# The exps of each block's first right chunk in two column parts

## The reference

```
xn   = group_norm(x)                       # 32 groups
g_x  = g_w @ xn + g_b                      # 128 channels, transposed to (n, 128)
f    = einsum('bnc,bcm->bnm', xn^T, xn)    # 4096 x 4096, symmetric
attn = softmax(f, axis=-1)
y    = attn @ g_x
wy   = W_w @ y + W_b
wy   = batch_norm(wy) * gamma + beta       # statistics over all 4 images
out  = x + (wy + xn)
```

## Time and profile before

| | |
|---|---|
| median of 3 runs | 2335.37 us (2332.52 to 2337.6) |
| the profiled execution's own time | 2335.4 us |
| its span, from first to last instruction | 2333.3 us |
| mean granted TensorE clock | 0.988 of full speed |
| PE busy | 2146.0 us, 92% |
| DVE busy | 1714.3 us, 73% |
| ACT busy | 1084.3 us, 46% |
| POOL busy | 904.7 us, 39% |

### The profile page before, as it was taken

One profiled execution on the slowest core, in us unless ns is written; L12 is line 12 of the kernel. 1 busy time (PEld: TensorE's weight loads), 2 busy tenths in 40 slices (PEclk: granted clock), 3 DMA queues, 4 the chain that ended last, 5 costly groups with the idle time before them and its releaser, 6 DMA issues.

```text
span 2333.3 us, 32462 instructions
## 1 busy us (share of the span) xinstructions
PE 2146.0 (92%) x9520; PEld 1507.4 (65%) x9520; DVE 1714.3 (73%) x3062; ACT 1084.3 (46%) x2206; POOL 904.7 (39%) x624
## 2 busy tenths in 40 slices
PE   5899999998999999998999999999899999999778
PEld 4787777654587776654568777765458777665323
DVE  5466667888856767788866666788985677777876
ACT  3344554454434454546444455445444444554435
POOL 3011224568601023459631122446860102346860
PEclk9899999999999999999999999999999999999999
DMA  3121233535412323454421223353441232346859
GB/s 134 71 95 73 102 107 118 194 113 169 147 43 87 112 87 113 149 172 136 162 68 80 89 86 119 122 193 114 160 156 51 77 113 93 107 142 205 297 203 360
DMA packets 108407, 304.55 MB, mean 131 GB/s; under 512 B 11456, under 2 KB 11968, under 8 KB 93888
## 3 DMA queue, kind: packets, MB, share of 16 engines
q1 hardware_dynamic: 108224, 302.37, 38.1%
HBM read 159.71 MB, written 142.61 MB: 130 GB/s over the span
## 4 chain that ended last, share of the span: by engine, by line
PE 63%; POOL 16%; issue 11%; DVE 5%; ACT 3%; DMA 2%; SPq 0%; DVEq 0%; POOLq 0%; ACTq 0%
PE bank L1109 9%; PE bank L1168 9%; PE bank L1111 9%; PE bank L1110 9%; PE bank L1144 8%; POOL fy_d L682 6%; POOL fy_c L682 6%; PE bank L1172 4%; PE bank L1174 4%; PE bank L1173 4%; PE bank L1304 2%; POOL xl L655 2%; PE bank L1234 2%; ACT ring L748 2%; DVE lacc L963 2%
## 5 line engine op out<-in xcount | busy, mean ns | idle before, releaser
L774 ACT CAST phi<-bank 128x512 fp32r<-128x512 f32 x480 | 280.4, 586 | 838.6 <-PE bank L1144 837.9
L911 DVE TENSOR_SCALAR_CACHE_REDUCE ring<-bank 128x512 f32<-128x512 f32 x576 | 395.5, 687 | 255.3 <-PE bank L1111 252.8
L1109 PE MATMUL bank<-xh 128*128 128x512 f32 x1152 | 541.2, 470 | 7.2 <-POOL xl L655 6.4
L1111 PE MATMUL bank<-xh,xl 128*128 128x512 f32 x1152 | 455.1, 395 | 0.0
L1110 PE MATMUL bank<-xl,xh 128*128 128x512 f32 x1152 | 452.3, 393 | 0.0
L946 DVE TENSOR_TENSOR plo<-bank,phi 128x512 fp32r<-128x512 f32 x480 | 325.6, 684 | 141.1 <-ACT phi L774 98.0
L1144 PEld LDWEIGHTS bank<-ident,ring 128*128 128x128 f32 x1920 | 234.0, 142 | 191.7 <-issue 126.2
L682 POOL TENSOR_TENSOR fy_c<-fy_c,maxrow 128x512 f32<-128x512 f32 x200 | 299.7, 1500 | 148.3 <-DMA fy_c<-spill 148.3
L682 POOL TENSOR_TENSOR fy_d<-fy_d,maxrow 128x512 f32<-128x512 f32 x188 | 280.9, 1497 | 193.6 <-DMA fy_d<-spill 193.6
L748 ACT ACTIVATE ring<-ring,nmax 128x512 f32<-128x512 f32 x480 | 344.5, 719 | 0.0
L1144 PE MATMUL bank<-ident,ring 128*128 128x128 f32 x1920 | 295.4, 277 | 52.3 <-ACT ring L748 24.2
(11 more groups left out here) (109 smaller groups left out, 2921.5 us busy)
## 6 DMA issues: line engine op xcount, KB each, us to landing
spill<-ring SPq DMA_DIRECT2D x112, 1024.0 KB, 4.4
fy_c<-spill SPq DMA_DIRECT2D x200, 256.0 KB, 4.3
fy_d<-spill SPq DMA_DIRECT2D x188, 256.0 KB, 4.3
ring<-x_dram SPq DMA_DIRECT2D x40, 512.0 KB, 4.5
lbuf<-spill SPq DMA_DIRECT2D x60, 256.0 KB, 3.7
yd<-yn SPq DMA_DIRECT2D x32, 256.0 KB, 3.2
fx_a<-x_dram SPq DMA_DIRECT2D x16, 512.0 KB, 6.7
out_dram<-fx_a SPq DMA_DIRECT2D x16, 512.0 KB, 4.4
```

What stands on the lines that cost most here:

```text
L774: nc.scalar.copy(phi[:, HI_BUF[n], :], whole(p)).then_inc(hi_made, 1)
L911: last = nc.vector.tensor_scalar(ring[:, SLOT[u], t, :], src, 1.0, None, ALU.mult, ALU.max, accum_out=rowm[:, t, c:c + 1])
L1109: nc.tensor.matmul(dst, xh[:, k, rows], xh[:, k, cols], start=(k == 0), stop=False)
L1111: last = nc.tensor.matmul(dst, xl[:, k, rows], xh[:, k, cols], start=False, stop=(k == K - 1))
```

## The change

The four exps of a block's first right chunk are issued in two column parts. Where the plan has the exp of row tile 0, all four row tiles' first 128 columns (the columns of tile r = 0) are now issued, four ACTIVATEs of 128x128; the other 384 columns of each row tile stay at the step that the plan gave it, behind them. Exps of later chunks stay whole, and are issued ahead of the parts within a step. The `turn` of tile r = 0 of such a chunk waits only for the four exps of 128 columns; the turns of r = 1 to 3 wait for those of 384 columns. The row sums of the second part go to a further column of `rsum`, which `sum_right` adds with the others (its slice is open at the end). All other work keeps its place in every engine's order.

```diff
+def first_right(j):
+    return j + 1 if turned_self(j, j) else j
...
-EXPS_AT = {s: [x for x in PRODUCTS if EXP_STEP.get(x) == s] for s in range(FIRST_EXP, TILES)}
-EXP_NO = {x: n for n, x in enumerate(x for s in range(FIRST_EXP, TILES) for x in EXPS_AT[s])}
+def exp_parts(s):
+    here = [x for x in PRODUCTS if EXP_STEP.get(x) == s]
+    whole = [(*x, slice(0, W)) for x in here if x[1] > first_right(x[0])]
+    opened = [x for x in here if x[1] == first_right(x[0])]
+    return whole, opened
+
+EXPS_AT = {}
+for _s in range(FIRST_EXP, TILES):
+    _whole, _opened = exp_parts(_s)
+    EXPS_AT.setdefault(_s, []).extend(_whole)
+    if _opened and _opened[0][2] == 0:
+        EXPS_AT[_s] += [(*_opened[0][:2], t, slice(0, P)) for t in range(T)]
+    EXPS_AT[_s] += [(*x, slice(P, W)) for x in _opened]
+EXP_NO = {(*x[:3], x[3].start): n for n, x in enumerate(x for s in range(FIRST_EXP, TILES) for x in EXPS_AT[s])}
...
+def exp_count(j, c, r):
+    start = 0 if c > first_right(j) or r == 0 else P
+    return max(EXP_NO[j, c, t, start] for t in range(T)) + 1
...
-        rsum = sb("rsum", [P, 2, T, NB])
+        rsum = sb("rsum", [P, 2, T, NB + 1])
...
-            def exp_right(b, j, c, t):
+            def exp_right(b, j, c, t, cols):
-                if t == 0:
+                if t == 0 and cols.start == 0:
                     act.wait_ge(max_made, b * NB + j + 1)
...
-                nc.scalar.activation(ring[:, SLOT[u], t, :], ring[:, SLOT[u], t, :], ACT.Exp,
-                                     bias=nmax[:, j % 3, t:t + 1], accum_out=rsum[:, j % 2, t, c:c + 1]
+                into = NB if cols.start else c
+                nc.scalar.activation(ring[:, SLOT[u], t, cols], ring[:, SLOT[u], t, cols], ACT.Exp,
+                                     bias=nmax[:, j % 3, t:t + 1], accum_out=rsum[:, j % 2, t, into:into + 1]
                                      ).then_inc(right_exp, 1)
...
-                pe.wait_ge(right_exp, b * NEXP + max(EXP_NO[j, c, t] for t in range(T)) + 1)
+                pe.wait_ge(right_exp, b * NEXP + exp_count(j, c, r))
```

## The result

The changed kernel is slower: 2395.7 us, where 2374 was forecast and 2390 was the upper end of the range. The ratio to the kernel before is 1.0252, 95% interval 1.0229 to 1.0274, or 59 us on 2336.3 us (the medians of the comparison). One of its four executions was in a slower state (3631.2 us at a mean clock of 0.555), which the median of 2395.7 counts and the ratio leaves out; the other three took 2391.9, 2393.7 and 2397.8 us. The profiled execution took 2391.9 us with a span of 2390.0 us, 56.7 us longer than before.

What follows compares the result with a forecast made beforehand. PE, busy 92% of the span, was taken as the bound, so time counts only where PE idles. 2335.4 + 24.6 (delays behind ACT's split exps) + 14.0 (clock) = 2374 us; range 2352 to 2390 us.

Steps and rivals of the forecast that it cites:

- the place: Starts of blocks 1 to 3: first turn 1.3 us earlier, but second turn, waiting for `plo`, 1.12 us later.
- the price of a part: On ACT, splitting an exp costs 0.28 us more per row tile, 1.12 us per chunk; ends 0.13 and 0.38 us.
- the delays: Later casts and `plo` at block starts: 13.4 + 4.9 + 3.8 + 2.5 = 24.6 us.
- Nothing, in eight places: Starts of blocks 5 and 7: ACT's idling before the next cast hides the added 1.22 us, so no delay.
- the clock's term: Starts of blocks 1 to 4: PE's joined idling of 2.5 to 2.9 us drops the clock, costing 14.0 us.
- I take two thirds of the 16, 11 drops, at 1.27 us: Blocks 1 to 4: 11 of 16 starts drop to 1.2 GHz, each costing 1.27 us, 14.0 us in all.
- My upper bound, 16 x 1.8 = 29 us: Clock loss at most: all 16 starts of blocks 1 to 4 drop, each at 1.8 us, dearest against cheapest stretch.
- Rival 1: Starts of blocks 1 to 4: slower by the 24.6 us, but the clock keeps up; 2360 us; chance 0.22.
- Rival 3: Part price at its upper end (34 us), nearly all 16 places lose the clock (29 us): 2398 us; chance 0.07.
- Rival 2: Part price near its lower end (11 us) and the clock holds: 2346 us; chance 0.08.
- rival 4: Faster: PE's 24.2 us of waiting for exps go, its `plo` waits don't grow: 2318 us; chance 0.04.
- rival 5: Effects cancel, or delays vanish in DVE's and POOL's waits in later blocks: 2335 us; chance 0.03.

Runs made afterwards that it cites:

- e8: Kernel before, whole exps, plus four one-column exps behind each first chunk's exps and unused matmuls where PE idles at blocks 1 to 4: 2361.3 us, ratio 1.0102.
- e3: Changed kernel plus ten unused 512-column matmuls on PE where it idles at each start of blocks 1 to 4: 2362.0 us, ratio 1.0094.
- e7: Changed kernel with the split only in blocks 5 and 7, whole exps elsewhere: 2341.7 us, ratio 1.0014 to the kernel before.
- e4: Changed kernel with ACT's cast of tile -1 (block 4: -2 and -1) moved ahead of the long parts, behind the short: 2359.6 us, ratio 1.0084.
- e2: Kernel before, whole exps, plus four one-column exps with accumulator behind the exps of each first chunk: 2382.1 us, ratio 1.0166.
- e1: Changed kernel, split kept, but the turn of tile 0 waits for all eight parts again: 2388.3 us, ratio 1.0203.

## Why the prediction was wrong

**Right: the place.** That the second turn and not the first sets the start of a block, that the wait for exps would turn into a wait for `plo`, and that the idling would be one stretch of 2.5 to 2.9 us: measured 2.65 to 2.81 (2.74 in most of blocks 1 to 3, 2.72 in most of block 4). The row of waits for `plo` reached 58.6 us, "over 50" as said; that for exps 9.7.

**Right: the price of a part.** 0.28 us from a difference of rows; e8 measured 0.28, the short and long exps 0.39 and 0.60 as worked out.

**Right in the main: the delays.** 24.6 us against 22 us in e3 (0.94%, interval 15 to 29 us) and 24 us in e8. Block by block, e3's marks move by 1.0 to 1.1 us at block 2, 0.8 to 1.1 at block 3 (1.12 forecast) and 1.1 at block 4 (1.22). In the changed kernel block 6 moves by 0.9 to 1.0 us in three images (1.12) and by 0.3 in the last (0.4), and the start of block 0 in the first image by 1.12 us, for 1.1. Its start between images can't be told from the clock's drops around it. Blocks 5 and 7 cost nothing at seven of eight starts, as e7 shows. "Nothing, in eight places" was wrong for one: block 7 of the last image costs 1.1 us. The idling of ACT that was to hide it had been read in another image.

**Wrong: the clock's term, 14.0 us.** The step "I take two thirds of the 16, 11 drops, at 1.27 us" failed on both factors, most on the second. There were 15 drops. Together they cost 34 us net (37 by the ratios), 2.2 us each. Counted by their length, 85 us at half clock, it would be 43 us; but e3, which lacks them, had 55 us of 1.2 GHz elsewhere and the changed kernel 42, so 2.2 us is if anything low.

I had read 1.27 us from two stretches that end with block 1's first exp. In both began a drop of 3.4 us, with PE busy all through it (start:end, length, busy us of five engines, granted clock, DMA):

```profile
181.47:184.88 3.41, 3.41 (x16) 3.01 (x15) 1.14 (x2) 1.69 (x5) 0.00 (x0) 0.50 0.01 5
737.84:741.25 3.41, 3.41 (x16) 3.02 (x15) 0.86 (x2) 0.58 (x1) 0.00 (x0) 0.50 0.02 7
```

The second cost 1.6 to 1.8 us, about half its length. The first cost 0.7 to 0.9: my row ended at 183.71, with 1.2 us of the low clock still to come, and what PE lost in these was taken up by its wait for the exps, 0.94 us before the first turn in place of 1.83. Behind the second turn of a block there is no such wait: PE was busy 6.80 us of 6.80 in the changed kernel's drop from 268.2, and 9.54 of 10.20 in that from 1968.0, and low clock cost up to half of its length. I also held a drop to be one short stretch; seven of 15 lasted 6.8 or 10.2 us. My upper bound, 16 x 1.8 = 29 us, was therefore no bound. With it and my price for the parts the sum would have been 2389 us, inside the range; with 34 us it is 2394. So the upper end of the range rested on the same step.

**The rivals.** Rival 1 (the clock keeps up) is what e3 made by hand, at 2362 us for 2360; it isn't what the chip did. The Trainium skill, in "TensorE: Matmul & The Clock Gate", its rules for kernel authors ("Why this matters for your kernels"), ties the fall of the clock to a longer gap than PE had here; the traces don't agree, with 15 drops at 16 stretches of 2.65 to 2.81 us in the changed kernel and four at 12 places of 1.5 us in e4. Rival 3 came nearest in time (2398), with the wrong reason for half of it: it needed 34 us from the parts, which cost 24. Rival 2 fell with the price, rival 4 with the row of waits for `plo`, which grew, and rival 5 with e3, where the delay stays with the clock up.

## What to carry to other kernels

Before splitting an instruction to release one waiter sooner, look at what stands behind it in its own engine's queue and at the waiter's next wait: here ACT owed PE a cast as well, each second part pushed it back by 0.28 us, and reordering what PE asks for, with the cast earlier too (1% gained), did what a quicker first answer did not. Price idle time of TensorE in front of dense work at more than its length: here 1.1 us more of it at each of 16 places cost another 34 us in clock, 2.1 us a place.

## What the runs showed of the hardware

A drop of the granted clock to 1.2 GHz did not always end with the first work behind it: it lasted 3.4 us in eight of 15 cases, and up to 10.2 us, with PE busy 9.54 us of them. Filling 2.3 us of PE's 2.74 us of idling with matmuls that nobody reads took away all 15 drops, and with them 34 us; in e8, where the fills stand in two idle stretches, the 1.2 GHz at these places went as well. How much idling is one too many is not settled by these runs. At places of the same length some dropped and some did not (e4, e2), and the same 2.72 us (2.65 in the last image) in front of block 4 brought three drops of four in the changed kernel and one of four in e1, while 2.61 us there in e2 brought none. An ACTIVATE with an accumulator on one column holds ACT for 0.28 us, so two of them on 128 and 384 columns cost 0.99 us for 0.71.
